# Three fused transformer phases on one core: feature-phase norms spread over more slots, and the work at the two phase borders split and moved

## The chip, the cores and the metric

The kernel runs on one core of a Trainium2 chip. The metric is the device time of one execution in microseconds (us). Each engine (PE for matmuls, DVE for vector work, ACT for activations, POOL, and SP, which here only issues transfers) has an instruction stream of its own in program order, and the streams are tied by semaphores: an instruction that waits holds up all that stands behind it in its stream.

## The reference

Three blocks run one after the other, all in float32 on 16 sequences of 256 tokens of width 128 (4096 tokens):

- **Features attention** (`L0_attn`): x2 = layernorm(x), used twice over (q and k are made of a layer norm, cosine and sine of `q @ proj` are the features); `kv = features(k)^T v`, `attn = features(q) kv`; then `x + attn @ wo`, a layer norm, and a two-matrix ReLU network of width 512.
- **Six layers** of windowed attention (`L0_ffn`): `q, k, v = x @ Wqkv`, unit length and rotary factors for q and k, softmax in windows of 32 with one window of look-back, `Wo`, and a gated GELU network.
- **Experts** (`L1_attn`, `L1_ffn`): a linear attention with elu+1, a layer norm, and the two best of eight expert networks, of width 512 each.

## The kernel before, in words

`build` calls three functions: `features_phase`, `layers_phase`, `experts_phase`. Each opens a block with one hand-written stream per engine. A block ends when its streams have ended; the next block starts only then.

**features_phase** (L946 to L1568). The tokens are 8 blocks (i) of 512. Each block has 16 slots (u = 0 to 15); in each, one pair of angle matmuls is made two slots ahead (`angles(U + 2)`), rounded by ACT in even slots and DVE in odd ones (`round_pair`), turned to a fraction and its absolute value by DVE (`fraction`), and turned to sine and cosine by ACT (`sines`). Into these slots the rest is written by hand: the layer norm of block i+1 (names norm_, bank NB `f_ps_norm`) and the second half of block i-1, "the tail" (names tail_, bank G `f_ps_tail`). The steps of the norms that matter here, with their slots:

- DVE, slot 5: `newton`, eleven dependent small operations (L1440 to L1450) that give 12 reciprocal square roots, 4 for each of three sets (two for the norm of block i+1, one for the tail of block i-1).
- DVE, slot 6: `diags`, three multiplications (L1459) that spread the roots on diagonal matrices 0, 1, 2.
- PE, slots 7 and 8: `norm_rows(1)`, `tail_rows` (L1178), `norm_rows(0)` (L1074) broadcast a diagonal by a matmul with ones. PE's wait for `norm_rows` is for two diagonals, for `tail_rows` for three.
- DVE: `norm_out(1)` slot 7 (`f_x_normed`), `tail_normed` slot 7 (`f_y_normed`), `norm_out(0)` slot 8 (`stream`, L1468).
- ACT: `norm_affine` slot 7, `tail_affine` slot 8 (L1327), `k_out` slot 9 (L1301), `kv_out`, then `tail_relu(0)` in slot 9 (L1333).
- PE, slot 9: `project_k` (L1080), which reuses bank NB, then `tail_hidden(0)` (L1186), which reads what `tail_affine` wrote.

Before block 0 there is a prologue: DVE waits for the constants, prepares the projection and clears three tables (L1389 to L1396, semaphore `setup` up to 9); PE and ACT wait for all nine; then the norm of block 0 is made with nothing beside it. Its k and q are stored as high and low parts and copied by 16 transfers each (`stack_k`, `stack_q`, on SP's queue) before the first angles. After block 7 the last tail runs with nothing beside it: PE and ACT alternate over the four parts of the ReLU layer, all through bank G (`tail_hidden`, `tail_relu`), and `tail_out` (L1192) waits for all four.

**layers_phase** (L67 to L926). SP issues the loads of the first layer's weights (`RAW`, 1664 KB), rotary table, mask and identity. POOL clears `V2` and `KD` (L699, L700). DVE waits for the constants, makes `IDR` from the identity (L709), a few small tables, then `tables(0)` and `divide(0, x)` for x = 0, 1, 2 (q, k, v): each a copy to the high part (L725) and a subtraction to the low part (L727). PE waits for all six before its first matmul.

**experts_phase** (L1633 to L2048). Eight blocks of 512 tokens. `attention(0, t)` runs alone first. Then each `turn(i)` runs 32 slots of expert matmuls with the steps of `attention(i + 1, t)` between them. Between `attention(0)` and `turn(0)` DVE divides the experts' first matrices into high and low parts (`split_w_in`, L2044 and L2046, 4096 columns each), and PE waits for both.

## Time and profile before

| | us |
|---|---|
| median of 3 runs | 4585.16 |
| lowest and highest | 4578.57, 4586.0 |
| the profiled execution's own time | 4581.09 |
| its span, first to last instruction | 4579.3 |
| granted TensorE clock, mean | 0.967 |

In the profile, the features phase takes the first 541 us, the layers phase 541 to 3939, the experts phase the rest. A line of the timeline gives start and duration in us, engine, line of the kernel, operation, output and inputs, shapes and count; in brackets stands how long the engine had been idle before it, and what ended that idle time. PEld is PE's weight load. A mean clock of 1.00 is 2.4 GHz, 0.50 is 1.2 GHz.

### The profile page before, as it was taken

Reading aid. Unit: us, or ns where it says so; the run is one execution under the profiler, and the core shown is the slowest. Engines: PE = TensorE matmul, PEld = TensorE weight load, DVE = VectorE, ACT = ScalarE, POOL = GpSimd, SP = SyncE. Lnnn points to the kernel's source line nnn. Section 1 sums busy time; section 2 is a strip of 40 time slices with the busy share of each in tenths; the row PEclk is TensorE's granted clock in tenths of the full one; section 3 lists DMA queues with packets and bytes.
Section 4 is the critical chain, followed back from the end, with each engine's and each line's share of the span. In section 5 each row is a group of like instructions: output and inputs, shape, how many; then the busy total and the mean of one; then the engine's idle time right before and its main releaser. Section 6 shows DMA issues by size and latency. Waiting matters only on the chain. (4 is left out here: it accounts for less than half of the span.)

```text
span 4579.3 us, 117809 instructions
## 1 busy us (share of the span) xinstructions
PE 4241.1 (93%) x44769; PEld 3404.5 (74%) x44769; DVE 3668.6 (80%) x6454; ACT 3143.1 (69%) x4910; POOL 1787.3 (39%) x966
## 2 busy tenths in 40 slices
PE   5888589999999999999999999999999999499999
PEld 2434268887888878888788887888788888387878
DVE  6888588888888888888888888888888887555653
ACT  5888367776777767777677777777777777133433
POOL 0000165554555545555455555555555554000000
PEclk9999799999999999999999999999999999699999
DMA  2111122222322323232332233223233223100000
GB/s 66 42 42 42 49 68 66 66 69 60 95 66 65 72 70 83 63 70 68 80 72 66 68 71 81 69 66 72 65 83 72 66 68 72 47 8 10 5 7 5
DMA packets 343226, 271.55 MB, mean 59 GB/s; under 512 B 231320, under 2 KB 236064, under 8 KB 341536
## 3 DMA queue, kind: packets, MB, share of 16 engines
q1 hardware_dynamic: 342688, 264.25, 24.3%
q8 instruction: 353, 5.78, 0.5%
q14 instruction: 185, 1.52, 0.1%
HBM read 29.23 MB, written 4.19 MB: 7 GB/s over the span
## 5 line engine op out<-in xcount | busy, mean ns | idle before, releaser
L672 POOL TENSOR_TENSOR qk_rotated<-qk_rotated,rotary_sines 128x1024 f32<-128x1024 f32 x384 | 923.1, 2404 | 1519.0 <-DVE rotary_sines L759 1519.0
L683 POOL TENSOR_TENSOR qk_rotated<-qk_rotated,rnorm 128x1024 f32<-128x1024 f32 x384 | 733.2, 1910 | 7.4
L767 DVE TENSOR_REDUCE qk_sumsq<-qk_squared 128x16 f32<-128x1024 f32 x384 | 466.4, 1215 | 159.2 <-ACT qk_squared L512 159.1
L231 PE MATMUL ps_proj<-qkv_w_hi,x_shifted_hi 128*128 128x512 f32 x1152 | 510.6, 443 | 16.3 <-DVE rotary_sines L759 12.7
L519 ACT ACTIVATE q_t<-ps_qk_t 128x512 f32<-128x512 f32 x384 | 229.3, 597 | 380.1 <-PE ps_qk_t L287 370.4
L749 DVE TENSOR_TENSOR qk_rotated<-ps_proj,rotary_scaled 128x1024 f32<-128x1024 f32 x384 | 467.5, 1217 | 7.0 <-ACT qk_squared L512 6.9
L759 DVE TENSOR_TENSOR rotary_sines<-ps_proj,rotary_scaled 128x1024 f32<-128x1024 f32 x384 | 466.2, 1214 | 1.4 <-POOL qk_rotated L672 1.4
L533 ACT ACTIVATE k_t_by_head<-ps_qk_t 64x512 f32<-64x512 f32 x768 | 452.2, 589 | 10.9 <-PE ps_qk_t L296 1.5
L233 PE MATMUL ps_proj<-qkv_w_hi,x_shifted_lo 128*128 128x512 f32 x1152 | 459.0, 398 | 0.0
L232 PE MATMUL ps_proj<-qkv_w_lo,x_shifted_hi 128*128 128x512 f32 x1152 | 456.1, 396 | 0.0
L312 PE MATMUL ps_scores<-k_t_by_head,q_t 128*32 128x128 f32 x12288 | 415.0, 276 | 9.7 <-ACT ps_scores L542 5.1
L512 ACT ACTIVATE qk_squared<-ps_proj 128x1024 f32<-128x1024 f32 x384 | 393.1, 1024 | 32.9 <-DVE qk_sumsq L767 14.3
L564 ACT ACTIVATE attn_out_t<-ps_attention 128x512 f32<-128x512 f32 x384 | 228.9, 596 | 264.6 <-PE ps_attention L350 264.6
L341 PE MATMUL ps_attention<-v_by_window,probs_t 128*32 128x128 f32 x12288 | 408.2, 273 | 1.3 <-ACT probs_t L557 1.3
L1874 ACT ACTIVATE e_hidden<-e_ps_hidden,e_b_in 128x512 f32<-128x512 f32 x256 | 175.2, 687 | 337.0 <-PE e_ps_hidden L1829 336.9
L312 PEld LDWEIGHTS ps_scores<-k_t_by_head,q_t 128*32 128x32 f32 x12288 | 312.2, 109 | 94.7 <-issue 87.0
L341 PEld LDWEIGHTS ps_attention<-v_by_window,probs_t 128*32 128x32 f32 x12288 | 329.7, 110 | 22.3 <-ACT probs_t L557 19.2
L773 DVE TENSOR_REDUCE neg_max<-ps_scores 128x8 fp32r<-128x512 f32 x384 | 263.4, 686 | 67.1 <-PE ps_scores L312 50.2
L789 DVE TENSOR_TENSOR attn_out<-ps_attention,row_rsum 128x512 f32<-128x512 f32 x384 | 264.4, 688 | 35.8 <-PE ps_attention L341 35.8
L1818 PEld LDWEIGHTS e_ps_expert<-e_w_out,e_hidden 128*128 128x128 f32 x2048 | 263.6, 191 | 19.9 <-ACT e_hidden L1874 0.3
L231 PEld LDWEIGHTS ps_proj<-qkv_w_hi,x_shifted_hi 128*128 128x128 f32 x1152 | 220.8, 192 | 69.4 <-DVE rotary_sines L759 38.4
L1818 PE MATMUL e_ps_expert<-e_w_out,e_hidden 128*128 128x128 f32 x2048 | 265.8, 275 | 0.0
(251 smaller groups left out, 9483.7 us busy)
## 6 DMA issues: line engine op xcount, KB each, us to landing
v_by_window<-v_tokens SPq DMA_DIRECT2D x1152, 128.0 KB, 2.4
v_by_window<-v_tokens SPq DMA_DIRECT2D x384, 64.0 KB, 2.1
k_t_by_head<-k_t_by_head SPq DMA_DIRECT2D x96, 256.0 KB, 4.3
v_by_window<-v_by_window SPq DMA_DIRECT2D x192, 64.0 KB, 2.0
qkv_w_raw<-in_layer_qk_dram SPq DMA_DIRECT2D x7, 1664.0 KB, 8.5
f_k_stacked<-f_k_hi SPq DMA_DIRECT2D x64, 64.0 KB, 2.0
f_k_stacked<-f_k_lo SPq DMA_DIRECT2D x64, 64.0 KB, 2.0
f_q_stacked<-f_q_hi SPq DMA_DIRECT2D x64, 64.0 KB, 2.0
```

The costliest lines, as they stand in the source:

```text
L231: mm(out, hi, HI[:, o:o + 512], start=True, stop=False)
L232: mm(out, hi, LO[:, o:o + 512], start=False, stop=False)
L233: last = mm(out, lo, HI[:, o:o + 512], start=False, stop=True)
L312: last = mm(S[WIN * w:WIN * w + WIN, c * P:(c + 1) * P], QT[:, 4 * g.half + c, q:q + WIN], KD[:, :, 4 * g.half + c, k:k + 2 * WIN], start= ...
L341: last = mm(A[WIN * w:WIN * w + WIN, o:o + P], PT[:, o + WIN * w:o + WIN * w + WIN], V2[:, 4 * g.t + w, :, 4 * g.half + c, :], start=True, ...
L533: a(KD[r, h, 4 * g.half:4 * g.half + 4, base:base + P], TP[r, :].rearrange("p (c k) -> p c k", k=P), ACT.Copy).then_inc(kt_out, 1)
L672: tt(u, u, TB[:], ALU.add).then_inc(added, 1)
L683: tt(u, u, r.unsqueeze(3).broadcast_to((P, 2, 8, DH)), ALU.mult).then_inc(scaled, 1)
L749: tt(U[m.p][:, t, x, :].rearrange("p (h e) -> p h e", e=DH), PJ[b][:].rearrange("p (h e) -> p h e", e=DH), cos, ALU.mult).then_inc(rot, 1)
L759: tt(TB[:].rearrange("p (h a b) -> p h a b", a=2, b=DH // 2), swapped(b), sin, ALU.mult).then_inc(rot, 1)
L767: nc.vector.reduce_sum(SS[:, 16 * i:16 * i + 16], SQ[:].rearrange("p (h e) -> p h e", e=DH), AX).then_inc(sumsq, 1)
L1818: last = mm(YB[e % 2][:, chunk(c)], H[:, e % 2, m, chunk(c)], WO[:, e, m, :], start=(m == 0), stop=(m == HM - 1))
```

## The change

Five groups of edits; nothing that is computed changes.

1. **Features, slots.** `newton` does six of its steps in slot 5 and five in slot 6. `diags` makes matrix 1 in slot 6, 2 in slot 7, 0 in slot 8, and PE's waits count one, two and three of them. `tail_rows` and `tail_normed` move from slot 7 to 8, `tail_affine` from 8 to 9. The semaphores of k and q parts are merged (`kq_hi`, `kq_lo`).
2. **Features, prologue.** PE, ACT and DVE start when three small tables are written; the projection's preparation and the three clearings come after `norm_out(0, 0)`, ahead of `k_low(0)`. ACT runs one sine on a column first. SP's queue gets the load of `RAW` behind the loads of x.
3. **Features, last tail.** The four parts of the ReLU layer use four banks; `tail_out` waits for them one by one.
4. **Border to the layers.** `RAW` is allocated outside both phases. POOL makes the low part of x first and clears `V2` behind it. `KD` is cleared by ACT. DVE divides q and k first, then waits for the constants, makes `IDR` and the tables, and divides v. PE waits for each part where it is used.
5. **Border to the experts.** ACT writes the high part (`WIHI`) in `attention(0, 3)`; DVE makes the low part expert by expert, two before `turn(0)` and six in its slots 0, 4, ..., 20.

```diff
@@ features_phase, sync @@
+            sp.dma_start(RAW[:], qk_first).then_inc(raw_in, 16)
@@ features_phase, tensor @@
-                pe.wait_ge(diag, 3 * b + 2)
+                pe.wait_ge(diag, 3 * b + (1 if k == 1 else 3))
-                pe.wait_ge(diag, 3 * chains(q + 1) + 3)
+                pe.wait_ge(diag, 3 * chains(q + 1) + 2)
+            return (G, NB, KV, AB)[k] if q == NBLK - 1 else G
-                else:
+                elif q < NBLK - 1:
                     pe.wait_ge(h_out, 4 * q + k)
-                mm(G[:], W[:, A_W1 + k * P:A_W1 + (k + 1) * P], YN[:], start=True, stop=True).then_inc(h_mm, 1)
+                mm(hidden_bank(q, k)[:], W[:, A_W1 + k * P:A_W1 + (k + 1) * P], YN[:], start=True, stop=True).then_inc(h_mm, 1)
-                pe.wait_ge(h_out, 4 * q + 4)
+                if q < NBLK - 1:
+                    pe.wait_ge(h_out, 4 * q + 4)
                 for k in range(4):
+                    if q == NBLK - 1:
+                        pe.wait_ge(h_out, 4 * q + k + 1)
-            pe.wait_ge(setup, NSETUP)
+            pe.wait_ge(setup, 3)
-                        if u == 7:
+                        if u == 8:
                             tail_rows(q)
@@ features_phase, scalar @@
-            act.wait_ge(setup, NSETUP)
+            act.wait_ge(setup, 3)
+            a(WARM[:], HALFPI[:], ACT.Sin)
+            norm_sq(0)
             act.wait_ge(c_in, 48)
-            norm_sq(0)
-                        if u == 8:
+                        if u == 9:
                             tail_affine(q)
@@ features_phase, vector @@
-            dve.wait_ge(c_in, 48)
-            ts(PB[:], PB[:], float(1.0 / (np.sqrt(RD) * 2 * np.pi)), None, ALU.mult).then_inc(setup, 1)
...
-            nc.vector.memset(KVP[:], 0.0).then_inc(setup, 1)
-            dve.wait_ge(setup, NSETUP)
+            dve.wait_ge(setup, 3)
-            newton(0, 0, None)
-            diags(0)
+            newton(0, 0, None, range(CHAIN))
+            dve.wait_ge(c_in, 48)
+            for k in (1, 2, 0):
+                diags(0, k)
             norm_out(0, 1)
             norm_out(0, 0)
+            ts(PB[:], PB[:], float(1.0 / (np.sqrt(RD) * 2 * np.pi)), None, ALU.mult).then_inc(setup, 1)
...
+            nc.vector.memset(KVP[:], 0.0).then_inc(setup, 1)
             k_low(0)
                     if u == 5:
-                        newton(i + 1, i + 1 if nxt else None, q if i > 0 else None)
+                        newton(i + 1, i + 1 if nxt else None, q if i > 0 else None, range(0, 6))
                     if u == 6:
-                        diags(i + 1)
+                        newton(i + 1, i + 1 if nxt else None, q if i > 0 else None, range(6, CHAIN))
+                        diags(i + 1, 1)
+                    if u == 7:
+                        diags(i + 1, 2)
+                    if u == 8:
+                        diags(i + 1, 0)
-                        if u == 7:
+                        if u == 8:
                             tail_normed(q)
@@ layers_phase @@
-            sp.dma_start(RAW[:], layer_qk[0]).then_inc(raw_in, 16)
+                pe.wait_ge(split, 2)
-            pe.wait_ge(split, 6)
+            pe.wait_ge(kd_zero, 1)
+                a(KD[:].rearrange("p h c k -> p (h c) k"), ZS[:, 0:1].unsqueeze(2).broadcast_to((P, 16, KW)), ACT.Copy).then_inc(kd_zero, 1)
                 low_part(Batch(0, 0), (setup, 0))
+                nc.gpsimd.memset(V2[:], 0.0).then_inc(v2_zero, 1)
-            nc.gpsimd.memset(V2[:], 0.0).then_inc(setup, 1)
-            nc.gpsimd.memset(KD[:], 0.0).then_inc(setup, 1)
+            divide(0, 0, proj_v, 0)
+            divide(0, 1, proj_v, 0)
+            dve.wait_ge(const_in, 48)
+            cp(IDR[:], IDENT[:]).then_inc(setup, 1)
+            dve.wait_ge(setup, NSETUP)
             tables(0)
-            for x in range(3):
-                divide(0, x, proj_v, 0)
+            divide(0, 2, proj_v, 0)
@@ experts_phase @@
+                if t == 3 and isinstance(i, int) and i == 0:
+                    act.wait_ge(experts_in, 32)
+                    a(WIHI[:], WI[:], ACT.Copy).then_inc(wi_high, 1)
+            def w_in_low(e):
+                dve.wait_ge(wi_high, 1)
+                tt(WILO[:, e, :], WI[:, e, :], WIHI[:, e, :].bitcast(F32), ALU.subtract).then_inc(wi_low, 1)
+                    if m == 0 and e < E_ - 2 and isinstance(i, int) and i == 0:
+                        w_in_low(e + 2)
-                pe.wait_ge(wi_split, 2)
+                pe.wait_ge(wi_high, 1)
-                cp(WIHI[:], WI[:]).then_inc(wi_split, 1)
-                tt(WILO[:], WI[:], WIHI[:].bitcast(F32), ALU.subtract).then_inc(wi_split, 1)
```

## Rows read from the trace of the kernel before

**Rows 1.** The page: busy time of each engine, share, instructions.
```profile
PE 4241.1 (93%) x44769; PEld 3404.5 (74%) x44769; DVE 3668.6 (80%) x6454; ACT 3143.1 (69%) x4910; POOL 1787.3 (39%) x966
```
**Rows 2.** Stretches: length, busy and count by engine, granted clock, DMA share, GB/s.
```profile
279.00:337.00 58.00, 47.43 (x349) 23.37 (x348) 50.81 (x72) 47.43 (x58) 0.00 (x0) 0.91 0.17 39
...
600.00:3939.00 3339.00, 3250.53 (x38494) 2720.80 (x38494) 2853.72 (x4934) 2522.47 (x4105) 1752.37 (x947) 0.99 0.30 70
```
**Rows 3.** Timeline of the prologue, 0 to 50 us.
```profile
7.19 0.43 DVE L1389 TENSOR_SCALAR f_proj_blocks<-f_proj_blocks 128x512 f32<-128x512 f32 x1 [6.15 <-DMA f_ident<-in_ident_dram]
...
15.39 2.08 PE L1058 MATMUL f_ps_norm<-f_x,f_mean_sel 128*128 128x512 f32 x2 [15.39 <-DVE f_kv L1396]
...
18.37 1.28 ACT L1286 ACT_TABLE_LOAD   x1 [18.37 <-DVE f_centered L1415]
...
24.78 1.89 DVE L1459 TENSOR_TENSOR f_rstd_diag<-f_ident,f_rnorm 128x512 f32<-128x512 f32 x3
...
31.16 0.69 DVE L1468 TENSOR_TENSOR stream<-f_centered,f_ps_norm 128x512 f32<-128x512 f32 x1 [2.23 <-PE f_ps_norm L1074]
...
34.75 0.75 DVE L1474 SCALAR_TENSOR_TENSOR f_k_lo<-f_ps_norm,f_w,f_k_hi 128x512 fp32r<-128x512 f32 x1 [2.91 <-ACT f_k_hi L1301]
...
47.15 2.08 PE L1109 MATMUL f_ps_angle<-f_proj_stacked,f_k_stacked 128*128 128x512 f32 x4 [5.76 <-DMA f_k_stacked<-f_k_lo]
```
**Rows 4.** The load of x's block 0, issued at 0.75 us: time to landing.
```profile
DMA to landing us min/median/max: 3.1/3.1/3.1
```
**Rows 5.** Timeline of block 1 of the features, slots 5 to 9.
```profile
123.89 1.22 DVE L1402 TENSOR_SCALAR f_rounded<-f_ps_angle 128x1024 f32<-128x1024 f32 x1
...
127.01 1.89 DVE L1459 TENSOR_TENSOR f_rstd_diag<-f_ident,f_rnorm 128x512 f32<-128x512 f32 x3
128.81 1.21 DVE L1408 SCALAR_TENSOR_TENSOR f_fraction<-f_rounded,f_ps_angle 128x1024 f32<-128x1024 f32 x1
...
135.00 1.13 PE L1074 MATMUL f_ps_norm<-f_rstd_diag,f_mean_sel 128*128 128x512 f32 x2
135.43 0.80 ACT L1327 ACTIVATE f_y_normed<-f_y_normed,f_w 128x512 f32<-128x512 f32 x1
136.91 1.13 PE L1080 MATMUL f_ps_norm<-f_x_normed,f_w 128*128 128x512 f32 x2
139.02 0.68 ACT L1301 ACTIVATE f_k_hi<-f_ps_norm,f_w 128x512 fp32r<-128x512 f32 x1
139.91 0.71 ACT L1333 ACTIVATE f_hidden<-f_ps_tail,f_w 128x512 f32<-128x512 f32 x1
```
**Rows 6.** The clock in two stretches of block 1 (columns as in Rows 2).
```profile
126.40:133.00 6.60, 5.74 (x12) 2.31 (x16) 5.75 (x9) 3.71 (x4) 0.00 (x0) 0.52 0.00 0
133.00:137.00 4.00, 3.90 (x39) 1.95 (x39) 3.59 (x4) 3.03 (x5) 0.00 (x0) 0.95 0.00 0
```
**Rows 7.** Timeline of the last tail of the features.
```profile
518.87 2.08 PE L1186 MATMUL f_ps_tail<-f_y_normed,f_w 128*128 128x512 f32 x2 [1.62 <-ACT f_y_normed L1327]
...
530.28 6.62 PE L1192 MATMUL f_ps_tail<-f_hidden,f_w 128*128 128x512 f32 x8 [0.78 <-ACT f_hidden L1333]
```
**Rows 8.** Timeline of the border from the features to the layers.
```profile
540.94 6.92 POOL L699 MEMSET v_by_window<- 128x8192 f32 x1 [540.48 <-POOLq L946]
547.80 4.36 POOL L700 MEMSET k_t_by_head<- 128x5120 f32 x1
549.33 2.91 DVE L709 CAST ident_r<-ident 128x128 fp32r<-128x128 f32 x1 [10.91 <-DMA ident<-in_ident_dram]
554.20 1.63 DVE L727 TENSOR_TENSOR qkv_w_lo<-qkv_w_raw,qkv_w_hi 128x1024 fp32r<-128x1024 f32 x1
560.14 0.76 PE L490 MATMUL ps_scores<-ident_r 128*128 128x512 f32 x1 [23.24 <-DVE qkv_w_lo L727]
```
**Rows 9.** Timeline of the border between attention(0) and turn(0) of the experts.
```profile
4001.11 2.29 DVE L2044 CAST e_w_in_hi<-e_w_in 128x4096 fp32r<-128x4096 f32 x1
4007.95 0.77 PE L1805 MATMUL e_ps_v<-e_ident,e_attn_t 128*128 128x128 f32 x2 [16.99 <-DVE e_w_in_lo L2046]
```

More of the change, by code:

```diff
@@ L64, in __init__, with layers_phase @@
         self.n, self.live = self.m.n * 4 + self.k, self.m.live
-def layers_phase(nc, layer_qk, layer_w, consts, XF):
+def layers_phase(nc, layer_qk, layer_w, consts, XF, RAW, raw_in):
     ctx = ExitStack()
@@ L77, in layers_phase @@
         W = sb("layer_w", [P, LW])
-        RAW = sb("qkv_w_raw", [P, RAWW])
         HI, LO = sb("qkv_w_hi", [P, QKVW], F32R), sb("qkv_w_lo", [P, QKVW], F32R)
@@ L433, in turn @@
                 shift(gs[0])
+                if j == -1:
+                    pe.wait_ge(split, 4)
                 if j == B - 1 and more(layer):
@@ L450, in turn @@
                 k_t(gt[1])
-                if j == 3 and (not isinstance(layer, int) or layer > 0):
+                if j == 3:
                     pe.wait_ge(w_in, layer * 16 + 16)
@@ L616, in turn @@
                 exps(gs[1])
-                if j == 3 and (not isinstance(layer, int) or layer > 0):
+                if j == 3:
                     act.wait_ge(w_in, layer * 16 + 16)
@@ L940, with features_phase @@
 PAIRS = 16
-def features_phase(nc, xT, attn_w, consts, XF, x_attn):
+def features_phase(nc, xT, attn_w, consts, XF, x_attn, qk_first, RAW, raw_in):
     ctx = ExitStack()
@@ L1427, in tail_args, with newton @@
                 ts(ARG[:, 8:12], G[:, 0:8].rearrange("p (c u) -> p c u", u=2)[:, :, 0], 1.0 / (D * D), 1e-5 / (D * D), ALU.mult, ALU.add).then_inc(t_arg, 1)
-            def newton(n, b, q):
-                if b is not None:
+            def newton(n, b, q, steps):
+                if b is not None and 0 in steps:
                     dve.wait_ge(n_arg, 2 * b + 2)
-                if q is not None:
+                if q is not None and 0 in steps:
                     dve.wait_ge(t_arg, q + 1)
                 yi = YR[:].bitcast(I32)
-                for k in range(CHAIN):
+                for k in steps:
                     if k > 0:
@@ L1457, in diags @@
                 after(dve, t_bc, n - 2)
-                for k in range(3):
-                    tt(DG[:, k], IDENT[:].unsqueeze(1).broadcast_to((P, 4, P)), RN[:, 4 * k:4 * k + 4].unsqueeze(2).broadcast_to((P, 4, P)),
-                       ALU.mult).then_inc(diag, 1)
+                tt(DG[:, k], IDENT[:].unsqueeze(1).broadcast_to((P, 4, P)), RN[:, 4 * k:4 * k + 4].unsqueeze(2).broadcast_to((P, 4, P)),
+                   ALU.mult).then_inc(diag, 1)
             def norm_out(b, k):
@@ L1564, in _ @@
             tail_args(q)
-            newton(NBLK + 1, None, q)
-            diags(NBLK + 1)
+            newton(NBLK + 1, None, q, range(CHAIN))
+            for k in (1, 2, 0):
+                diags(NBLK + 1, k)
             tail_normed(q)
@@ L1693, in experts_phase @@
         NUM, DEN, GATE = KB, VB, KV
-        w_in_s, x_in, x_out, setup, xa_free, y_free, chain = (sem(x) for x in ("weights_in", "x_in", "x_out", "setup", "xa_free", "y_free", "chain"))
+        w_in_s, x_in, x_out, setup, y_free, chain = (sem(x) for x in ("weights_in", "x_in", "x_out", "setup", "y_free", "chain"))
         x1_done, q_mm, k_mm, v_mm, q_min, q_exp, k_min, k_exp, q_done, kv_in, kv_mm, kv_heads = (sem(x) for x in (
@@ L1824, in turn @@
                         pe.wait_ge(h_out, SLOTS * i + t - 1)
+                    if m == 0 and isinstance(i, int) and i == 0:
+                        pe.wait_ge(wi_low, e + 1)
                     mm(HB[t % 2][:], WIHI[:, e, chunk(m)], XHI[:], start=True, stop=False)
@@ L2039, in turn, with first_low @@
                 dve.wait_ge(y_acc, SLOTS * (i + 1))
-            def split_w_in():
-                dve.wait_ge(experts_in, 32)
-                cp(WIHI[:], WI[:]).then_inc(wi_split, 1)
-                dve.wait_ge(wi_split, 1)
-                tt(WILO[:], WI[:], WIHI[:].bitcast(F32), ALU.subtract).then_inc(wi_split, 1)
-            blocks(dve, attention, turn, split_w_in)
+            def first_low():
+                w_in_low(0)
+                w_in_low(1)
+            blocks(dve, attention, turn, first_low)
 HD1 = D // HEADS
```

84 lines of the change are left out of this document (45 added, 39 removed).

## The prediction, made before the changed kernel was run

> **What bounds the kernel now.** I read the page first: PE is busy for 93% of the span, DVE for 80% [rows 1], an average over three phases with different limits. So I cut the span into stretches. In the layers phase, 3339 us of it, PE is busy for 97% at full clock [rows 2]; the change touches nothing that repeats there, and I carry it over unchanged. In the features phase a block takes 58.0 us, of which DVE is busy 50.8, ACT 47.4 and PE 47.4 [rows 2]: none is full, so the order in which they wait for each other decides. The borders I read in the timeline, each as a chain with one engine at work. Nearly all that the change can give lies in four such places: the prologue, the last tail of the features, and the two borders. The fifth place, seven blocks of features, can take it back.
>
> **Prologue.** Before, PE's first matmul waits until 15.39 us for DVE's preparation and clearing, which runs from 7.19 to about 15.3, 8.1 us [rows 3]. After, it waits only for x's block 0, issued at 0.75 and landed 3.1 us later, at 3.85 [rows 4]; I take 3.9. From there the old chain is kept up to `norm_out(0, 0)`, which before ended 31.16 + 0.69 - 15.39 = 16.5 us after the first matmul [rows 3]. Two pieces leave it: the 1.28 us table load (ACT now does it early, for the sine on a column), and one of three diagonals, 1.89 / 3 = 0.63, since PE's first wait is for one and not two. That leaves 14.6, so it ends at 18.5. Then the 8.1 us of preparation, now on DVE in front of `k_low(0)`: 26.7 instead of 34.75, so 8.0 us earlier. All that follows (16 transfers of k on SP's queue, then the first angles at 47.15) hangs on `k_low` and moves with it. The load of `RAW` stands on SP's queue behind x's and ahead of the transfers of k; SP has issued it before 7 us and next has work at 27.5, so it has some 20 us where the same load needs 7 to 9. Term: **-8.0**. If x's block lands 2.5 us later, as the median of its eight loads does, it is -5.5; I see nothing that would bring more than -8.5.
>
> **The slots of the features (blocks 1 to 6).** Here is the main doubt. I walk through block 1 [rows 5], with DVE full in both versions. Before: `newton` ends at 123.9, rounding and fraction take 3.1, diagonals 1.8. After: six steps of `newton` end at 122.9; rounding and fraction 126.1; five steps and diagonal 1 at 127.8, 0.5 us ahead of before; fraction, diagonal 2 and `norm_out(1)` 1.9 + 0.6 + 0.6 at 130.9; rounding, fraction and diagonal 0 3.1 + 0.6 at 134.6. Now comes the stall: `norm_out(0)` stands directly behind diagonal 0, and needs PE's row matmul of it, 1.13 plus about 0.1 for the hand-over, so DVE waits some 1.2 us that it did not before. PE goes on with `tail_rows` (0.9 apart), the angles of slot 11 and two transposes (0.9 together), and `project_k` from 137.3 to 138.4 [spacing in rows 5]. ACT takes k's high part from 138.4 to 139.0, 0.6 ahead of before, then two copies (0.3), and then `tail_affine` (0.7), which before was done at 135.4, long ahead. It ends at 140.0; only then can PE make `tail_hidden(0)`, 1.2, and ACT, whose next instruction is `tail_relu(0)`, waits for it with nothing to do. That relu starts at 141.3; before it started at 139.91 [rows 5]. Behind it stand the next sines and the rounding that DVE needs, and ACT has no idle time from there to the end of slot 15. So +1.4 us a block, six times: **+8.4**. In the last block (no norm of a next block, so no stall on diagonal 0) the same walk gives 0.9 less than before; in block 0, which has no tail, 0.3 more. Together **+7.8**. From below: if the ACT wait is taken up later in the block and the smaller bursts on DVE help, it is 0, or a gain of up to 1 us in each of 7 blocks, -7. From above: half clock, below.
>
> **Last tail.** PE waits for two diagonals, not three: 0.63. The four parts of the ReLU layer follow each other in 11.4 us (518.87 to 530.28), since each waits for the relu of the one ahead [rows 7]. With four banks PE issues them back to back: 8 matmuls at the spacing of the 8 behind them, 6.62 / 8 = 0.83 each, are 6.6, and the relus lie beside. The last product then waits for the fourth relu (0.7) only behind three others. So 4.8 less 0.3 for hand-overs: 4.5. Term: **-5.1**. This stretch ran at 1.2 GHz; should the denser stream bring 2.4 GHz before its end, up to 4 more are won.
>
> **Border to the layers.** Call its start, 540.94, T. Before, PE's first matmul is at T + 19.2 [rows 8]: constants and clearing until T + 11.2, then tables and three divisions. One row is striking: the copy of the identity to `IDR`, 128 columns, has 2.91 us and ends at 552.24, when POOL's second clearing ends (552.16) [rows 8]. DVE's copy waited for POOL's running instruction. After the change POOL makes x's low part first (T + 1 to about T + 4) and then clears `V2` for 6.9 us, until about T + 11.2, just while DVE wants to make `IDR`. DVE has the first two divisions behind it by T + 6 or so; ACT clears `KD`, 5120 columns, beside it: its 512-column operations take 0.7 us with their fixed part [rows 5], so 7 us at most, done by T + 8. PE needs `IDR`, so it starts at about T + 12, not at T + 19.2; the tables and v's division end some 3 us later, still ahead of DVE's first rotary product, which also waits for q's projection and the squares. Term: **-7**. Bounds: if the second division too is caught behind the clearing, PE starts at T + 13, -6.2; if nothing is, at T + 6.4, -12.8. In the Trainium skill, "SBUF — State Buffer", section "SBUF: two separate sides", the port pair that the two engines share is an exclusive lock for a whole instruction, and a DVE instruction with two SBUF inputs conflicts only with a POOL instruction that reads SBUF. The copy's row agrees with the lock; by the second half the subtraction of the division would pass beside a clearing and only the copies be held, which is the -7; no row here shows such a subtraction beside a clearing.
>
> **Border to the experts.** PE stands idle for 17.0 us until DVE's division of the experts' matrices ends; the division starts at 4001.11, PE at 4007.95 [rows 9]. After, the high part is ACT's, made while ACT waits for the attention in any case; of the low part two experts (512 columns each) stand ahead of x's low part, and PE's first matmuls don't need them. PE starts at about 4001.25: 6.7 less. The other six parts, about 0.6 to 0.7 each, go to DVE slots in which it mostly waits for PE; I price one place, slot 8, where the norm's result comes 0.3 us ahead of PE's need: +0.4. Term: **-6.3**; at worst all six delay PE, -2.5.
>
> **Sum.** -8.0 + 7.8 - 5.1 - 7 - 6.3 = -18.6 against the profiled execution's 4581.09 is 4562.5. The median of the three runs is 4.1 above that execution, which would give 4566.6; the runs scatter over 7.4. I say 4565. A difference of 0.2%, 9.2 us, is about what a measurement of this kernel can tell from none.
>
> **Rivals.**
> - *The slots cost nothing or give something.* The four other terms stand alone, -26.4, and with a gain of 0 to 1 us in 7 blocks the time is 4552 to 4559. For it: DVE is the fullest engine, and the burst of newton and diagonals in slots 5 and 6 is what PE's angle matmuls wait behind. Against it: the walk, in which two results are asked for directly behind their source.
> - *Half clock in the new gap, slower than before.* In block 1 the granted clock is 0.52 from 126.4 to 133, after PE had idled, and 0.95 from 133 to 137 [rows 6]. The new order makes PE idle again just before diagonal 0. If the clock is at 1.2 GHz from there on, row matmul, `tail_rows`, angles, transposes and `project_k` take 3.1 us more until k's high part, `tail_hidden(0)` 0.95 more: +5.4 a block, +33 for six, about +3 for the other two. -26.4 + 36 is +10: 4595. It decides from 5.2 us a block over seven blocks on. For it: each block before has such a half-clock stretch. Against: it ends at 133, before the place. A milder form (half of the blocks, or some us of it) gives -5 to -10, 4575 to 4580.
> - *No conflict of POOL and DVE at the border.* 5.8 us less, 4559. Against it stands the copy's row.
> - *The prologue's head start is lost*, because SP's transfers of k are late behind `RAW` or the first load is: +3 to +5, 4569. SP's idle time of 20 us speaks against it.
>
> **Chances.** My walk with its own range of 4557 to 4574: 0.53. Slots at no cost or with a gain: 0.29. Half clock in its mild form 0.09, in its full form 0.03. The other two, or some loss in the experts' first turn, 0.06. Leaving about one in ten out on either side the range is 4549 to 4577. Faster by over 0.2% (under 4576): walk, free slots, small parts of the rest, 0.86; within: 0.10; slower: 0.04.
>
> **What would show it.** Prologue: first matmul at 3.9, first angles at 39.1. Slots: a block of 59.4 us and not 58.0; ACT idle about 1.3 us before `tail_relu(0)` and again before k's high part, DVE idle 1.2 before `stream`. Last tail: 6.6 us for the four parts instead of 11.4. Border: `IDR`'s copy ends with the clearing of `V2`, PE starts 12 us after the block. Experts: PE idles some 10 us ahead of `turn(0)`, not 17. The prediction is wrong if a block is shorter than 58.0, or longer than 61.

## The result and the profile after

| | before | after |
|---|---|---|
| median of 4 runs each, us | 4585.11 | 4557.56 |
| lowest and highest | 4578.57, 4586.0 | 4554.58, 4560.78 |
| profiled execution | 4581.09 | 4560.78 |
| its span | 4579.3 | 4559.0 |

The ratio is 0.9943, 95% interval 0.9926 to 0.996: faster by 0.4 to 0.7%. The forecast was 4565 with a range of 4549 to 4577. The measured median lies 7.4 us under the 4565, inside the range. The profiled executions differ by 20.3 us, the medians by 27.6: that of before ran 4.0 us under its median, and that of after is the slowest of its four, 3.2 over its median. The forecast's sum of 18.6 was made against the profiled execution of before, so it is compared with the 20.3. That agreement hides two things: at the five places of the change 28.7 us went, not 18.6, and 8.4 us came back behind them, nearly all in code that the change doesn't touch.

PE's share on the page of after is what it was [rows 1]:

```profile
PE 4238.4 (93%) x44769; PEld 3405.2 (75%) x44769; DVE 3669.8 (80%) x6460; ACT 3151.9 (69%) x4912; POOL 1782.6 (39%) x965
```

**Prologue.** The timeline of after, 0 to 50 us (columns as in [rows 3]):

```profile
0.75 1.28 ACT L1351 ACT_TABLE_LOAD   x1 [0.75 <-PEq L2181]
...
3.88 2.04 PE L1069 MATMUL f_ps_norm<-f_x,f_mean_sel 128*128 128x512 f32 x2 [3.88 <-DMA f_x<-in_x_dram]
...
17.71 0.69 DVE L1474 TENSOR_TENSOR stream<-f_centered,f_ps_norm 128x512 f32<-128x512 f32 x1 [2.23 <-PE f_ps_norm L1085]
...
26.49 0.75 DVE L1480 SCALAR_TENSOR_TENSOR f_k_lo<-f_ps_norm,f_w,f_k_hi 128x512 fp32r<-128x512 f32 x1
...
39.00 2.04 PE L1120 MATMUL f_ps_angle<-f_proj_stacked,f_k_stacked 128*128 128x512 f32 x4 [5.87 <-DMA f_k_stacked<-f_k_lo]
```

First matmul at 3.88 (forecast 3.9), first angles at 39.00 (39.1): 8.15 us earlier than in [rows 3].

**Slots.** The timeline of after in block 1, slots 8 and 9, DVE and ACT:

```profile
127.40 0.69 DVE L1474 TENSOR_TENSOR stream<-f_centered,f_ps_norm 128x512 f32<-128x512 f32 x1 [1.22 <-PE f_ps_norm L1085]
128.25 0.69 DVE L1509 TENSOR_TENSOR f_y_normed<-f_centered_tail,f_ps_tail 128x512 f32<-128x512 f32 x1 [0.17 <-PE f_ps_tail L1189]
```
```profile
129.79 0.69 ACT L1316 ACTIVATE f_k_hi<-f_ps_norm,f_w 128x512 fp32r<-128x512 f32 x1 [1.17 <-PE f_ps_norm L1091]
130.38 0.44 ACT L1328 ACTIVATE f_kv<-f_ps_attn 128x128 f32<-128x128 f32 x2
130.70 0.82 ACT L1342 ACTIVATE f_y_normed<-f_y_normed,f_w 128x512 f32<-128x512 f32 x1
132.73 0.69 ACT L1348 ACTIVATE f_hidden<-f_ps_tail,f_w 128x512 f32<-128x512 f32 x1 [1.22 <-PE f_ps_tail L1197]
```

The three idle times that the walk named are there, 1.22, 1.17 and 1.22 us; the two ACT rows have none in [rows 5], and `stream` had 0.19 us in block 1 of before:

```profile
136.17 0.69 DVE L1468 TENSOR_TENSOR stream<-f_centered,f_ps_norm 128x512 f32<-128x512 f32 x1 [0.19 <-PE f_ps_norm L1074]
```

Yet block 3 of after is shorter than that of before [rows 2], not longer. The stretch by windows (columns as in [rows 2]):

```profile
270.43:328.20 57.77, 46.04 (x349) 22.59 (x350) 50.62 (x72) 47.66 (x58) 0.00 (x0) 0.94 0.16 42
```

The granted clock is 0.94 over the block and 0.91 in [rows 2]; the experiments say why.

**Last tail.** PE in after:

```profile
513.11 2.07 PE L1197 MATMUL f_ps_tail<-f_y_normed,f_w 128*128 128x512 f32 x2 [1.63 <-ACT f_y_normed L1342]
514.98 1.91 PE L1197 MATMUL f_ps_norm<-f_y_normed,f_w 128*128 128x512 f32 x2
516.69 1.17 PE L1197 MATMUL f_ps_kv<-f_y_normed,f_w 128*128 128x512 f32 x2
517.69 1.02 PE L1197 MATMUL f_ps_attn<-f_y_normed,f_w 128*128 128x512 f32 x2
518.55 3.60 PE L1206 MATMUL f_ps_tail<-f_hidden,f_w 128*128 128x512 f32 x8
```

The four parts take 5.4 us (518.55 - 513.11), not 11.4 as in [rows 7], and the product 3.60 and not 6.62: two matmuls take 2.07 at the start and 1.02 at the end, so 1.2 GHz turned into 2.4 GHz within the four parts.

**Border to the layers**, after (T, the start of the block, is 526.3):

```profile
529.06 6.92 POOL L694 MEMSET v_by_window<- 128x8192 f32 x1
```
```profile
528.54 1.54 DVE L729 TENSOR_TENSOR qkv_w_lo<-qkv_w_raw,qkv_w_hi 128x1024 fp32r<-128x1024 f32 x1
530.01 6.52 DVE L727 CAST qkv_w_hi<-qkv_w_raw 128x1024 fp32r<-128x1024 f32 x1
536.56 1.22 DVE L729 TENSOR_TENSOR qkv_w_lo<-qkv_w_raw,qkv_w_hi 128x1024 fp32r<-128x1024 f32 x1
537.71 0.22 DVE L928 CAST ident_r<-ident 128x128 fp32r<-128x128 f32 x1
...
538.69 0.69 DVE L727 CAST qkv_w_hi<-qkv_w_raw 128x1024 fp32r<-128x1024 f32 x1
```
```profile
538.03 0.77 PE L494 MATMUL ps_scores<-ident_r 128*128 128x512 f32 x1 [15.88 <-DVE ident_r L928]
```

PE starts at T + 11.8 (forecast T + 12; before T + 19.2 [rows 8]). It wasn't `IDR`'s copy that waited for the clearing of `V2`, but the copy of k's high part, one instruction earlier: 6.52 us where the same copy of v takes 0.69. It ends 0.5 us behind the clearing.

**Border to the experts**, after:

```profile
3981.33 0.77 PE L1828 MATMUL e_ps_v<-e_ident,e_attn_t 128*128 128x128 f32 x2 [10.37 <-DVE e_attn_t L2042]
```

PE idles 10.37 us, not 16.99 [rows 9]. The head start at this point is 26.6 us (4007.95 - 3981.33); at the end it is 20.3.

**The balance**, read at the same instruction of both traces. A feature block is measured here from ACT's copy of one block's attention to the next:

| stretch | before | after | difference | forecast |
|---|---|---|---|---|
| to the first angles | 47.15 | 39.00 | -8.15 | -8.0 |
| block 0 | 58.90 | 58.75 | -0.15 | +0.3 |
| blocks 1 to 6 | 346.29 | 347.41 | +1.12 | +8.4 |
| block 7 | 52.15 | 53.36 | +1.21 | -0.9 |
| last tail, to T | 36.45 | 27.8 | -8.65 | -5.1 |
| T to the first v_tokens | 39.4 | 31.9 | -7.5 | -7 |
| layers from there on | | | +2.1 | 0 |
| border to the experts | | | -6.6 | -6.3 |
| experts' turns and end | | | +6.3 | 0 |

### The profile page after: what moved, and what is told of

Its sections match the earlier page's. It is cut to its first block and busy times, and to the rows that moved or that the text cites. A ratio compares the mean times of both kernels' runs of the same rounds, so it can differ in the third digit from the quotient of the medians.

```text
span 4559.0 us, 117845 instructions
## 1 busy us (share of the span) xinstructions
PE 4238.4 (93%) x44769; PEld 3405.2 (75%) x44769; DVE 3669.8 (80%) x6460; ACT 3151.9 (69%) x4912; POOL 1782.6 (39%) x965
## 5 line engine op out<-in xcount | busy, mean ns | idle before, releaser
L537 ACT ACTIVATE k_t_by_head<-ps_qk_t 64x512 f32<-64x512 f32 x768 | 452.2, 589 | 10.4 <-PE ps_qk_t L295 1.0
L340 PEld LDWEIGHTS ps_attention<-v_by_window,probs_t 128*32 128x32 f32 x12288 | 329.9, 110 | 22.1 <-ACT probs_t L561 19.2
L670 POOL TENSOR_TENSOR x_shifted_lo<-stream,x_shifted_hi 64x256 fp32r<-64x256 f32 x96 | 69.7, 726 | 535.6 <-ACT x_shifted_hi L509 526.8
```

Source lines behind the costliest of these rows:

```text
L340: last = mm(A[WIN * w:WIN * w + WIN, o:o + P], PT[:, o + WIN * w:o + WIN * w + WIN], V2[:, 4 * g.t + w, :, 4 * g.half + c, :], start=True, ...
L537: a(KD[r, h, 4 * g.half:4 * g.half + 4, base:base + P], TP[r, :].rearrange("p (c k) -> p c k", k=P), ACT.Copy).then_inc(kt_out, 1)
```

## Experiments

Each kernel was timed in five rounds (eleven runs of e1, five of each other) beside the kernel before; e1 to e4, e5 to e8, and e9 to e11 ran on one chip each. Ratios are to before; the differences in the text are of the medians of runs beside each other, or of positions in the traces, as said.

| run | median us | ratio, 95% interval |
|---|---|---|
| e1 | 4590.8 (before 4585.05) | 1.0014, 1.0005 to 1.0023 |
| e2 | 4554.75 | 0.9935, 0.992 to 0.9949 |
| e3 | 4556.36 | 0.9937, 0.9923 to 0.9951 |
| e4 | 4568.96 | 0.9964, 0.9951 to 0.9978 |
| e5 | 4558.71 (before 4585.57) | 0.9942, 0.9928 to 0.9955 |
| e6 | 4553.68 | 0.9926, 0.9913 to 0.994 |
| e7 | 4563.59 | 0.9951, 0.9937 to 0.9965 |
| e8 | 4548.8 | 0.9923, 0.991 to 0.9937 |
| e9 | 4555.14 (before 4582.35) | 0.9933, 0.992 to 0.9947 |
| e10 | 4555.25 | 0.994, 0.9926 to 0.9953 |
| e11 | 4543.9 | 0.9918, 0.9905 to 0.9932 |
| e12 | 4546.11 (before 4584.34) | 0.9916, 0.9903 to 0.993 |

### Slots: e1, e2, e12 and e3

e1 is before with the slots' edits alone, e2 is after without them (the merged semaphores of k and q apart, which e1 lacks and e2 keeps):

```diff
-                        newton(..., range(0, 6))
+                        newton(..., range(CHAIN))
                     if u == 6:
-                        newton(..., range(6, CHAIN))
-                        diags(i + 1, 1)
-                    if u == 7:
-                        diags(i + 1, 2)
-                    if u == 8:
-                        diags(i + 1, 0)
+                        for k in range(3):
+                            diags(i + 1, k)
```
(and `tail_rows`, `tail_normed` in slot 7, `tail_affine` in slot 8, with PE's waits for two and three diagonals).

> The kernel before with the second kind of edit alone in its seven feature blocks: newton in two slots, the three diagonals in three, tail_rows, tail_normed and tail_affine one slot on. Prologue, last tail and both borders are those of before. Theory A (what the two traces suggest): the waits that the walk named cost 1.1 to 1.4 us a block (ACT before tail_relu(0) and before k's high part), and the smaller bursts of DVE take away a half-clock stretch in slots 2 to 5 that costs as much, so a block stays at 57.8 to 58.2 us and the whole is -3 to +4 us against before. In its trace, which has the old prologue, the granted clock in slots 2 to 5 is 1.00. Rival B (the walk alone): +1.4 us a block, +7.8 in all, and the stretch at half clock in slots 2 to 5 is still there, because only the start of the blocks in time had moved it. Rival C: the slots are a gain of their own, -5 or more.

> The kernel after with the slots of the seven feature blocks as before: newton in one slot, three diagonals in one, the tail's steps one slot earlier. Prologue, last tail and borders as after. Theory A: within 4 us of the kernel after, 4554 to 4562, a block of 57.8 to 58.2 us with a half-clock stretch in slots 2 to 5 again. Rival B (the walk alone): 7.8 us faster than after, 4550, a block of 56.4 to 57. Rival C (the slots are a gain): 5 us or more slower than after, 4563 and up.

The lengths of the blocks tell more than the total. Windows of e2, block 1 and block 3; then of e1, block 3 and block 6:

```profile
95.77:151.68 55.91, 45.58 (x349) 23.10 (x350) 49.71 (x71) 47.32 (x58) 0.00 (x0) 0.94 0.18 44
209.61:267.59 57.98, 47.45 (x349) 23.39 (x350) 50.79 (x72) 47.46 (x58) 0.00 (x0) 0.91 0.16 41
```
```profile
221.01:278.74 57.73, 46.16 (x349) 22.59 (x350) 50.58 (x72) 47.66 (x57) 0.00 (x0) 0.94 0.17 41
394.20:453.27 59.07, 47.42 (x348) 22.95 (x348) 50.66 (x72) 47.66 (x57) 0.00 (x0) 0.91 0.17 41
```

In windows of 3 us over each block one sees where the clock is at 1.2 GHz. With the old slots (before, e2, and the later e8, e11) block 1 has one such stretch, in about slots 6 to 8, a mean clock of 0.94 and 55.9 to 56.2 us; blocks 2 to 6 have a second one, in about slots 3 and 4, a mean of 0.91 and 57.9 to 58.2 us. With the new slots (after, e1, e10) block 1 has 57.15 us; four of blocks 2 to 6 have nothing in slots 3 and 4, a mean of 0.94 and 57.7 to 57.8; and one block has a second stretch and 59.1 to 59.2. So there are two effects:

- With the same clock pattern a block is 1.0 to 1.3 us longer with the new slots: block 1, and block 6 of e1, which has its two stretches where before has them and takes 59.07 for 58.0. This is the walk's +1.4, a little smaller.
- The new slots have a costly second stretch in one block of five, not in all five. Within e1 it is the difference between 57.73 and 59.07. That gives back what the waits cost.

The mean alone doesn't give a block's length; the place of the stretch counts. Block 1 of e10 has a mean of 0.97 and the same 57.16 us as after's with 0.94. And block 6 of e10, at half clock in slot 5 and again in slot 8, has 59.19 us at a mean of 0.94:

```profile
383.93:443.12 59.19, 46.27 (x348) 22.57 (x348) 50.56 (x72) 47.51 (x57) 0.00 (x0) 0.94 0.15 40
```

The windows in slots 3 and 4, in block 3 of before and then of e1, which has before's prologue and so nearly before's times:

```profile
229.19:232.19 3.00, 3.00 (x15) 1.04 (x17) 2.90 (x4) 3.00 (x4) 0.00 (x0) 0.50 0.00 0
```
```profile
230.01:233.01 3.00, 3.00 (x36) 1.23 (x34) 2.97 (x4) 3.00 (x4) 0.00 (x0) 1.00 0.00 0
```

PE gets through 15 matmuls in the one and 36 in the other. Rival B of e1 (the start of the blocks in time had moved the stretch) is refuted: the order of the slots takes it away. Which part of the new order the clock answers to was not shown. In its sum e1 missed theory A: at the border to the layers its trace stands 0.16 us ahead of before, but the time is 0.05 to 0.23% longer (2.3 to 10.5 us). In the traces the loss stands in code that e1 doesn't touch: 2.5 us up to the first matmul of `turn(0)`, 5 behind it. Since the medians show it too (5.75 us), it is hardly the luck of one execution; its cause is open. Rival C, a gain of 5 us or more from the slots alone, is refuted.

e2 is 0.5 us below e10 by the medians and 2.3 by the ratios (the two ran on different chips), with intervals that overlap; in the traces e2 gets from the first angles to the layers 3.3 us sooner than e10, whose block 0 has the same length as e2's (56.6 and 56.5). In this pair that is the slots' price, +3.3 instead of +7.8.

> The fastest kernel so far (4543.9 us: after with the old slots, clearings on POOL, V2's clearing behind the copy of v's high part) with one part of the slots' edit put back: newton does six steps in slot 5 and five in slot 6, and the three diagonals stand behind them in slot 6; norm_out, tail_rows, tail_normed and tail_affine keep the old slots. Theory A (the cost of the slots' edit is the two results asked for directly behind their source, ACT before tail_relu(0) and DVE before norm_out(0), which the spread of the diagonals and the moved tail make): the split of the root alone costs nothing of that kind, block 1 keeps 55.9 us (57.15 with the whole edit), and the kernel is within 3 us of 4543.9. Rival B (it is the later end of the root that makes all behind it late, since the fraction of slot 6 now stands ahead of its second half): block 1 gets 0.8 to 1.2 us longer, as with the whole edit, and the time is 1 to 8 us longer. Rival C (the smaller burst of DVE is what takes the half-clock stretch from slots 2 to 5): blocks 2 to 6 have one stretch and not two, and are 1 us or more shorter than 58.0.

```diff
-                        newton(i + 1, ..., range(CHAIN))
+                        newton(i + 1, ..., range(0, 6))
                     if u == 6:
+                        newton(i + 1, ..., range(6, CHAIN))
                         for k in range(3):
                             diags(i + 1, k)
```

Blocks 1 and 3 of e12:

```profile
92.85:149.09 56.24, 45.41 (x349) 23.00 (x350) 49.46 (x71) 47.33 (x57) 0.00 (x0) 0.94 0.17 43
207.19:265.25 58.06, 47.09 (x349) 23.31 (x350) 50.80 (x72) 47.45 (x58) 0.00 (x0) 0.91 0.16 40
```

Block 1 costs 0.3 us more than in e11 (55.93), not 1.2, and blocks 2 to 6 keep their second stretch. Theory A holds, B is refuted, and C too: both the waits and the better clock pattern come with the spread of the diagonals and the moved tail (no run parts these two), not with the division of the root.

> The kernel after with one ACT step moved: tail_relu(0) stands behind the two sines of slot 10, where it stood behind tail_affine in slot 9. ACT's 1.2 us of idle time before it has then two sines to fill it. Theory A: that wait is on the path, since ACT has no idle time from there to the end of slot 15; a block gets 1 to 1.2 us shorter and the time is 7 to 8 us under after, 4549 to 4551. Rival B: the time comes back as a wait of PE in slot 11 for the relu (tail_hidden(1) needs it) or of ACT before k's high part, and the kernel is within 2 us of after.

```diff
-                        if u in (9, 11, 13, 14):
-                            tail_relu(q, (9, 11, 13, 14).index(u))
+                        if u in (10, 11, 13, 14):
+                            tail_relu(q, (10, 11, 13, 14).index(u))
```

Blocks 1, 2 and 3 of e3:

```profile
98.72:155.10 56.38, 45.27 (x349) 22.66 (x350) 49.31 (x71) 47.55 (x58) 0.00 (x0) 0.94 0.17 43
155.10:213.56 58.46, 47.29 (x349) 23.17 (x350) 50.59 (x72) 47.53 (x58) 0.00 (x0) 0.91 0.16 41
213.56:270.53 56.97, 45.76 (x349) 22.65 (x350) 50.56 (x72) 47.65 (x58) 0.00 (x0) 0.94 0.17 43
```

ACT's wait of 1.22 us before `tail_relu(0)` is gone, and a block with one stretch is 0.77 us shorter (56.38 for 57.15, 56.97 for 57.75). The rest came back as a wait that after doesn't have, before q's high part:

```profile
138.39 0.69 ACT L1311 ACTIVATE f_q_hi<-f_ps_norm,f_w 128x512 fp32r<-128x512 f32 x1 [0.47 <-PE f_ps_norm L1097]
```

But now every second block (2, 4 and 6) has two stretches and 58.3 to 58.5 us, so blocks 1 to 6 together are only 1.7 us shorter than in e10. And block 0, in which `tail_relu` doesn't run, has 59.64 us here and 56.64 in e10, 3.0 more. The time is 1.1 us above e10's by the median and 1.4 below it by the ratio, so the 7 to 8 us did not come. Theory A was right on the wait and wrong on the time. Rival B was right that the time stays and that part of the wait moves to another place; the larger part went with the clock.

### Last tail: e4

```diff
-            return (G, NB, KV, AB)[k] if q == NBLK - 1 else G
+            return G
```
(and PE's waits for each relu as in the other blocks).

> The kernel after with the last tail's four parts of the ReLU layer through one bank again, each behind the relu of the one ahead, and the last product behind all four. Nothing else. Theory A: the four banks are worth more than the hand-overs because the denser stream of PE brings the clock from 1.2 to 2.4 GHz before its end: without them the clock is at 1.2 GHz again through the last product (6.6 us for 16 matmuls, as before, and not 3.6), and the time is 8 to 9 us above after, 4566. Rival B: the clock rises at the same moment whatever the order, since it rose in after for another reason; then only the hand-overs come back, 4.5 to 5.5 us, 4562.5.

PE in e4's last tail:

```profile
514.44 2.07 PE L1197 MATMUL f_ps_tail<-f_y_normed,f_w 128*128 128x512 f32 x2 [1.63 <-ACT f_y_normed L1339]
...
522.99 2.08 PE L1197 MATMUL f_ps_tail<-f_y_normed,f_w 128*128 128x512 f32 x2 [0.78 <-ACT f_hidden L1345]
525.85 6.71 PE L1203 MATMUL f_ps_tail<-f_hidden,f_w 128*128 128x512 f32 x8 [0.78 <-ACT f_hidden L1345]
```

Parts and product take 18.1 us here (514.44 to 532.56) and 9.0 in after (513.11 to 522.15): 9.1 more, 6.0 in the four parts and 3.1 in the product, with all at 1.2 GHz as before. Theory A holds: the rise belongs to the back-to-back order. The median is 11.4 above the first runs of after and the ratio 0.21 points (9.6 us), of which the tail is 9.1. The other traces agree: with one bank (before, e1, e4) the product takes 6.6 to 6.7 us, with four banks 3.6.

### Border to the layers: e5 and e9

```diff
-                nc.gpsimd.memset(V2[:], 0.0).then_inc(v2_zero, 1)
+                for k in range(16):
+                    nc.gpsimd.memset(v2[:, 512 * k:512 * k + 512], 0.0).then_inc(v2_zero, 1)
```

> The kernel after with POOL's clearing of V2 at the border to the layers (one instruction, 8192 columns, 6.92 us) cut into 16 instructions of 512 columns. Theory A (DVE's copy is held by POOL's running instruction and gets in when that one ends): the copy to k's high part takes at most 0.7 + 0.5 us instead of 6.52, IDR is ready some 6.5 to 7.5 us after the block's start T and PE's first matmul stands at T + 6.6 to T + 7.6, not T + 11.8; the first rotary product moves with it from T + 16.1 to about T + 11.5, and the time is 4 to 5 us under after. The subtraction of the division (two inputs in SBUF) stands beside the clearing then, and keeps 1.22 us. Rival B: POOL goes from piece to piece without a gap, so the copy gets in only behind the last: nothing changes, or it is some tenths worse. Rival C: the copy is short, but what sets PE's start is then the landing of the identity or the tables' constants, and less than 2 us come back.

e5, POOL and DVE (T is 525.6):

```profile
528.37 8.05 POOL L696 MEMSET v_by_window<- 128x512 f32 x16
```
```profile
529.32 1.05 DVE L729 CAST qkv_w_hi<-qkv_w_raw 128x1024 fp32r<-128x1024 f32 x1
530.40 1.23 DVE L731 TENSOR_TENSOR qkv_w_lo<-qkv_w_raw,qkv_w_hi 128x1024 fp32r<-128x1024 f32 x1
531.54 4.97 DVE L930 CAST ident_r<-ident 128x128 fp32r<-128x128 f32 x1
```

One copy slipped in between two pieces (1.05 us), the next, of 128 columns, was held 4.97 us until the last piece was done at 536.4. Theory A and rival B were both half right: a copy may get in between two pieces or be passed over by nearly ten of them. The subtraction beside the pieces kept 1.23. PE gained 0.8 us (T + 11.0); no gain in time can be told (the ratio is 0.9942, that of after 0.9943).

```diff
+                pool.wait_ge(split, 5)
                 nc.gpsimd.memset(V2[:], 0.0).then_inc(v2_zero, 1)
```

> The kernel after, with one wait more: POOL clears V2 only when DVE has copied v's high part (all three divisions' copies and IDR's are then behind DVE). Cut into 16 pieces, the clearing let k's copy in (1.05 us) but held IDR's 4.97 us. Theory A (a running clearing holds DVE's copies of SBUF, and nothing else): now no copy of DVE is held, k's copy and IDR's have 0.7 and 0.2 us, PE's first matmul stands at T + 6.5 and not T + 11.8, tables and v's division end at T + 9, the first rotary product stands at about T + 11 instead of T + 16.1; the clearing runs from about T + 7.5 to T + 14.4 beside v's subtraction and the rotary products, which keep 1.2 us each. The time is 4 to 5 us under after. Rival B: the identity or the rotary table has not landed yet at T + 6, so PE starts at T + 8 or later. Rival C: the clearing now delays POOL's first addition of rotary terms (it would be asked for at about T + 13.5), and half of the gain is lost there.

e9 (T is 526.4), DVE, POOL and PE:

```profile
531.99 0.22 DVE L929 CAST ident_r<-ident 128x128 fp32r<-128x128 f32 x1
...
532.97 0.69 DVE L728 CAST qkv_w_hi<-qkv_w_raw 128x1024 fp32r<-128x1024 f32 x1
533.70 1.23 DVE L730 TENSOR_TENSOR qkv_w_lo<-qkv_w_raw,qkv_w_hi 128x1024 fp32r<-128x1024 f32 x1
536.82 1.22 DVE L752 TENSOR_TENSOR qk_rotated<-ps_proj,rotary_scaled 128x1024 f32<-128x1024 f32 x1 [1.89 <-ACT qk_squared L516]
```
```profile
533.79 6.93 POOL L695 MEMSET v_by_window<- 128x8192 f32 x1 [4.66 <-DVE qkv_w_hi L728]
```
```profile
532.31 0.77 PE L494 MATMUL ps_scores<-ident_r 128*128 128x512 f32 x1 [10.04 <-DVE ident_r L929]
```

PE starts at T + 5.9, the first rotary product at T + 10.4; no copy is held, and v's subtraction beside the clearing keeps its 1.23. By the Trainium skill ("SBUF — State Buffer", section "SBUF: two separate sides") the port pair that the two engines share belongs, for its whole instruction, to whichever starts first among those that need it, and a DVE instruction with two SBUF inputs collides only with one of POOL that reads SBUF. The traces agree where POOL was first: copies held 6.52 and 4.97 us, subtractions beside a clearing 1.23, but 1.54 beside POOL's own subtraction (528.54 in after). The head start of 5.8 us at the first `v_tokens` doesn't arrive at the end: the layers from there to their last `v_tokens` take 3293.0 us, 2.5 more than in e10 (3290.5). The medians of e9 and e10 are equal, the ratios 3 us apart. The mechanism is shown, a gain in time is not.

### Prologue: e6

```diff
+        @block.gpsimd
+        def _(pool):
+            nc.gpsimd.memset(VP[:, 0], 0.0).then_inc(cleared, 1)
...
-            nc.vector.memset(VP[:, 0], 0.0).then_inc(setup, 1)
```

> The kernel after with the features' three clearings (the two halves of VP, and KVP; 2048 columns each, 1.76 us each on DVE) given to POOL, which does nothing in this phase, at its very start; PE, ACT and DVE wait for them where they waited for DVE's. Theory A: DVE goes from the preparation of the projection (ends at 19.9) straight to k_low(0), which waits for k's high part (ends at 21.3): it starts at 21.3 instead of 26.49 and the first angles are 5.2 us earlier, at 33.8; the time is 5 us under after. Rival B: q's projection and high part follow k_low as before, but the 16 transfers of k were already the longer leg and all moves with them; the same 5 us. Rival C: POOL's clearing takes the port from DVE's first operations, or is still running when the norm needs DVE, and 1 to 3 us are lost again.

`k_low(0)` starts at 21.64 instead of 26.49 and the first angles at 34.12 instead of 39.0 to 39.2, 5.1 us; the median is 1.6 us below that of e10 and the ratio 0.14 points, 6 us (different chips). DVE's first small clearing beside POOL's keeps 0.17 us. Theory A holds for the first angles; how much of the 5.1 us reaches the end can't be told from these runs alone. Block 0 takes 59.23 us here, 2.6 more than in e10.

### Border to the experts: e7

The experts phase of before in the kernel after.

> The kernel after with the whole experts phase of before: DVE makes high and low part in two instructions between attention(0) and turn(0). Theory A: PE's idle time ahead of turn(0) is 17 us again and not 10.4, the cost is the 6.6 us of the border less what the six low parts cost in turn 0 (0.4 to 0.9): 5.5 to 6.3 us above after. Rival B: the experts' turns run at one of two lengths (71.0 us where the granted clock dips once, 73.5 where it dips twice), and their number decides more than the border: a difference under 3 or over 9 us.

PE's idle time is 16.99 us again, the median is 6.0 above the first runs of after and the ratio 0.08 points (4 us). The idle time is shown; the time agrees with theory A, with intervals that overlap.

### Together, and after once more: e8, e10, e11

> The kernel after with the old slots of the feature blocks (3 to 4 us in its favour by the run with them), V2 cleared in 16 pieces (4 to 5) and the three clearings of the features on POOL (5). If the three add up: 12 to 14 us under after, 4544 to 4546. If the changed start of the blocks in time shifts the half-clock stretches so that a two-stretch block comes more often or the layers phase loses what it gains, 3 to 5 us less than that, 4548 to 4551.

> The kernel after, unchanged, on the same chip as the runs beside it. Both theories expect 4556 to 4561 us and a ratio of 0.994 to before. In its trace each feature block from 2 to 5 has one half-clock stretch and 57.75 us, and one block of the seven has two stretches and 59.1.

> The kernel after with the old slots of the feature blocks, the three clearings of the features on POOL, and V2's clearing behind the copy of v's high part. If the gains add up: 4 us under the run with all three edits that had V2 in 16 pieces (4548.8), 4544 to 4546. If the layers or the experts give some of it back by another pattern of half-clock stretches: 4546 to 4550.

e8 is in the range that it was given for gains partly lost. e11 is the fastest: its five runs (4541.8 to 4547.82) all lie under those of e10 on the same chip (4553.72 to 4559.21), by 11.4 us in the median. So the three edits together are a gain, also over after. e12 differs from it by one part and can't be told from it.

e10's ratio is the expected 0.994, its median 0.75 us under the range named. It shows how far the same program scatters. Block 0 in e10, then in after:

```profile
39.19:95.83 56.64, 41.91 (x325) 20.48 (x326) 50.94 (x69) 46.86 (x53) 0.00 (x0) 0.94 0.19 49
```
```profile
39.00:97.75 58.75, 42.82 (x325) 20.85 (x326) 50.93 (x69) 46.99 (x53) 0.00 (x0) 0.88 0.19 47
```

The same instructions, 2.1 us apart, with another granted clock.

## Why the prediction came out right, point by point

- **Prologue, -8.0.** Measured -8.15; each step as written. e6 shows that another 5.1 lay in the clearings, which the walk had counted as DVE's in any case.
- **Slots, +7.8.** This is the step that failed, in size, and by the prediction's own sign (a block shorter than 58.0: it is 57.77). The stalls are where it put them and cost 1.0 to 1.3 us in a block of the same clock pattern, for 1.4. But in before, blocks 2 to 6 have a second half-clock stretch in slots 3 and 4, and the new slots take it away in four of five (the fifth keeps it in e1, and has one in slot 8 in its place in after and e10). The sum is +2.2 in the profiled pair, +3.3 in the pair e2 and e10, and -0.2 in the traces of before and e1. Block 7 moves that sum by over 2 us: it is 1.2 us longer in after, but in e1, at a mean clock of 0.97, it is 51.17 us, 1.0 shorter, as the walk had it (0.9). The walk was made through block 1, the one full block of before without the second stretch: its 56.16 us beside the 58.0 of [rows 2] should have been the warning (0.6 of that difference is there with the new slots too, at the same mean clock). The bound from below had looked for a gain in ACT and DVE, not in the clock.
- **Last tail, -5.1.** Measured -8.65, e4 puts the four banks at 9.1. The mechanism was right, the term too small: "up to 4 more" if the denser stream brings 2.4 GHz stood there as a bound, and the value was taken at 1.2 GHz throughout. The 0.63 us of the diagonal's wait were won (PE idles 3.84 and not 4.44 us before the row matmul), and lost again in eight small matmuls ahead of it, which ran at 1.2 GHz (1.86 for 1.05).
- **Border to the layers, -7.** Measured -7.4 at PE's start and -7.5 at the first `v_tokens`. The price was right; which copy would be caught was not: k's, not `IDR`'s. So the second division was caught, for which the text had priced T + 13, -6.2, but only its copy. The bound from below, T + 6.4, is what e9 reached (T + 5.9).
- **Border to the experts, -6.3.** -6.6 at PE's start. The six low parts in turn 0 were taken at +0.4. Turn 0 takes 72.84 us in before and 73.78 in after, +0.9 (clocks 0.95 and 0.94), but the net price stays open: it has 71.3 to 71.7 us in e2, e3, e4, e8, e11 and e12, with the low parts, at a clock of 0.97 or 0.98.
- **Carried over unchanged: +8.4.** Layers and experts were taken at nothing, and gave back 2.1 and 6.3 us in the profiled pair (0.9 of it in turn 0). Turn 1 of the experts, before and then after:

```profile
4086.70:4157.70 71.00, 67.69 (x425) 57.94 (x426) 43.43 (x109) 27.73 (x41) 0.00 (x0) 0.98 0.03 9
```
```profile
4061.00:4134.40 73.40, 70.17 (x425) 59.33 (x425) 43.45 (x108) 27.75 (x41) 0.00 (x0) 0.94 0.03 8
```

  The same instructions take 71 us with one clock and 73.4 with the other. The profiled execution of before had two such fast turns of the first seven, that of after none; e1, with the experts phase of before, also none. The layers, first to last `v_tokens`, took 3287.7 us in before, 3290.6 in after, and 3290 to 3293.5 in the other runs. The profiled execution of before ran 4.0 us under its median and was in part a lucky one: the medians differ by 27.6 us, and against the 28.7 of the five places that leaves some 1 us given back, an estimate that takes those places as in the traces. But e1 lost 5.75 us by the medians, by its trace outside the features, so a change may move it; whether it can be steered was not shown.
- **Rivals.** "The slots cost nothing" came near (4552 to 4559 holds the median of 4557.56), though for a reason that it did not name: it had no loss in the slots, where the stalls cost what the clock gave. Half clock in the new gap did not come in most blocks: in block 3 of e10 the row matmul of diagonal 1 takes 2.07 us, and that of diagonal 0, behind it, 1.13, at 2.4 GHz: the stretch ends ahead of it. But it came in the one long block of after, block 6, as it did in e10 and e9. PE there:

```profile
415.04 2.07 PE L1085 MATMUL f_ps_norm<-f_rstd_diag,f_mean_sel 128*128 128x512 f32 x2 [3.05 <-DVE f_rstd_diag L1465]
```

  There DVE waits 2.17 us before `stream` and not 1.22, and the block is 1.4 us longer than its neighbours (59.20 for 57.76), where the rival had 5.4. The other two did not come either.

So in the profiled pair the sum came near, 20.3 for 18.6, because a cost put too high and gains put too low were met by a loss that was not in the sum. That is luck, and the median shows it: it fell by 27.6 us, and the 4565 was 7.4 too high.

## What to carry to other kernels

Walk through a block that is like the others: compare its length and granted clock with its neighbours first, since a block with another clock pattern can hide a cost or a gain. Where a removed wait makes TensorE's stream denser at 1.2 GHz, work out the term at both levels of the clock and ask which the new order will bring. And keep a long clearing on GpSimd away from VectorE's copies, by order and not by cutting it up.

## What the runs showed of the hardware that was not expected

- A VectorE copy held by GpSimd isn't served as soon as the next instruction boundary comes: beside 16 clearings of 0.5 us, one copy waited some 0.4 us and the next nearly 5 (e5). A clearing of VectorE itself beside one of GpSimd, and subtractions with two SBUF inputs, kept their times (0.17 and 1.23 us).
- The same program runs the same stretch at lengths that lie apart in steps: block 0 of the features 56.64 (mean clock 0.94), 58.75 (0.88) or 59.30 us (0.91; e10, after, e7, which are alike up to there), a turn of the experts 70.8 to 71.7 (0.97 or 0.98) or 72.8 to 73.8 (0.94 or 0.95). The mean clock alone doesn't order the lengths. A gain of a few us at one place can be taken back by such steps behind it, as in e3 and e9.
- Cutting one clearing of 6.92 us into 16 made it 8.05, 0.07 us for each cut.
